# Part of a query convolution in 32x32 array tiles: sixteen-tile matmuls, a score product in four column tiles, and new order tables

## The chip, the cores and the metric

The kernel runs on one core of one Trainium2 chip. The metric is the device time of that core in microseconds: the median of 3 runs before was 682.94 us (681.64 to 685.73). The engines are named as in the profile: PE (TensorE, with PEld for its weight loads), DVE (VectorE), ACT (ScalarE), POOL (GpSimd) and SP (SyncE, which issues the DMAs).

## What is computed

Two layers over 4 images of 256 channels and 32x32 points, all in fp32. The reference, cut:

```python
# layer 0, x: (4, 256, 32, 32)
qkv = conv1x1(x, wq | wk | wv)                       # 768 channels
dw = conv5x5(qkv, dw_kernel, groups=768)             # depthwise, 25 taps
pw = conv1x1(dw, pw_kernel, groups=96)               # 8x8 blocks
f = concat([qkv, pw]).reshape(B, -1, 24, N)          # 64 heads of 8
query, key_, value = relu(f[:, :, :8]), relu(f[:, :, 8:16]), f[:, :, 16:]
scores = einsum('bhdn,bhen->bhde', [value, 1], key_)
out = einsum('bhde,bhen->bhdn', scores, query)
out = out[:, :, :-1] / (out[:, :, -1:] + EPS)
x = batchnorm(conv1x1(out, proj)) + x
# layer 1
norm = (x - mean) / sqrt(var + EPS)
attention = softmax(conv1x1(norm, f_w).T @ conv1x1(norm, g_w))   # 1024 x 1024
out = conv1x1(conv1x1(x, h_w) @ attention.T, o_w) + x
```

## The kernel before

The order of every engine is written out by hand; semaphores tie the engines together, and nothing is scheduled at run time. 768 qkv channels are six **tiles** of 128 channels, one channel to a partition: tiles 0 and 1 are queries, 2 and 3 keys, 4 and 5 values. `raw` holds a tile's image with a border; `conv` is the depthwise result, 25 taps (multiply by one weight per channel, shift, add) of 1024 points a tile.

The depthwise convolution is shared. DVE does whole taps (`conv_taps`, L1226), each multiplied and added in one instruction into two banks of PSUM: tiles 2, 3 and 0, and a part of tile 1. For tiles 4 and 5 and the rest of tile 1, ACT makes a product (`conv_products`, L965) into one of five buffers `prod`, and POOL adds it (`conv_adds`, L1485). Tile 1 is the **shared tile**: its first ten taps (`LATE`) are added on POOL into a second sum (`late_of`, tile `rows` or `q_raw` in the rows) and are done last; seven more are done by POOL in `conv`, eight by DVE. In the first batch POOL takes twelve and DVE three, and PE does all 25 taps of tile 5 itself: `diagonal_conv` (L551), 25 matmuls of 128x128 diagonal weights for each half image of 512 points. DVE builds these weights (L1445).

A batch's `body(b)` on PE starts when conv of tiles 2 to 5 is ready: eight slots of grouped 1x1 products and transposes for keys and values (`pwkv`, L735 and L737), which ACT drains into `kt` and `vt` (L979, L980); then qkv of the next batch (`raw_kv`), the scores (`scores`, L561: 8 or 9 blocks, two halves h, a full 128x129 product of which a mask keeps the 8x8 blocks), the query part (`pwq`, L750 and, for the late sum, L754), the raw keys, values and queries of the next batch, the denominators (L580) and their spread (L602), the projection (L779), layer 1's statistics (POOL's `rstd`, L1479) and its folded weights (L702, L712, L826), and last the attention: eight rows of energy (L667), transposes (L682) and values (L691). The 25-tap convolution of batch b+1 fills DVE, ACT and POOL all the while; tables (`TAPS_...`, `PRODUCTS_...`, `LATES_...`, `RSTD_AT`, `CARRY`) say how many taps, products and adds stand between the steps of a body. `CARRY` taps of batch b stand at the start of body b.

PSUM has eight banks: 0 to 3 turn round as **A slots** (PE fills one, ACT drains it: `a_full`, `a_free`), 4 and 5 as **D slots** for DVE, 6 and 7 hold DVE's convolution sum. In the attention the A banks hold energies and transposes. An fp32 matmul of the program stands in the trace as two pairs of a weight load and a matmul.

## Time and profile before

| | us |
|---|---|
| median of 3 runs | 682.94 |
| profiled execution | 682.24 |
| its span | 680.5 |
| PE busy | 627.4 |
| DVE busy | 563.8 |
| POOL busy | 541.8 |
| ACT busy | 468.9 |

The span is from the first to the last instruction; 1.7 us of the profiled execution lie around it. Busy time is a union of instructions; for PE it holds the latency of each matmul as well as the time that it feeds the array, so that a PE read as busy may be a little less full. The stages used below are cut where body(b) starts its `pwkv` (the first L735 of the batch) and where the attention of a batch starts (its first L667).

### The profile page before, as it was taken

How to read it: one execution, taken by the hardware profiler on the slowest of the kernel's cores; microseconds unless marked ns; L12 is line 12 of the kernel's file. 1: busy time of each engine (PE TensorE's matmuls, PEld its weight loads, DVE VectorE, ACT ScalarE, POOL GpSimd, SP SyncE). 2: the span in 40 equal slices, each digit the busy share in tenths (PEclk: the TensorE clock that was granted, in tenths of full speed). 3: DMA queues.
4: the chain of work that ended last, by engine and by line, in shares of the span. 5: the costliest groups of instructions: out<-in, count | busy, mean ns of one | idle time of the engine just before them, and what ended most of it. 6: DMA issues, size and time to landing. Idle time of an engine off the chain costs nothing.

```text
span 680.5 us, 8641 instructions
## 1 busy us (share of the span) xinstructions
PE 627.4 (92%) x3176; PEld 471.1 (69%) x3176; DVE 563.8 (83%) x661; ACT 468.9 (69%) x741; POOL 541.8 (80%) x253
## 2 busy tenths in 40 slices
PE   4979988999989998999989998999988978899998
PEld 3844547665868787765868797756767866478886
DVE  5899899898899999988889999879899998373321
ACT  4797619897787669788777769788767864233331
POOL 4999997999999999989999899999999987010000
PEclk9989989999999999999989999999999999999999
DMA  8000001000010000001010000000100000000000
GB/s 306 1 0 1 0 0 63 1 1 27 36 63 15 17 17 15 1 1 62 6 58 15 17 23 9 0 1 1 43 20 16 16 16 15 1 1 0 17 16 31
DMA packets 6537, 16.23 MB, mean 24 GB/s; under 512 B 864, under 2 KB 992, under 8 KB 5984
## 3 DMA queue, kind: packets, MB, share of 16 engines
q1 hardware_dynamic: 6496, 15.69, 6.5%
q8 instruction: 25, 0.41, 0.3%
q14 instruction: 16, 0.13, 0.1%
HBM read 11.50 MB, written 4.19 MB: 23 GB/s over the span
## 4 chain that ended last, share of the span: by engine, by line
PE 35%; issue 20%; DVE 16%; POOL 15%; ACT 12%; DMA 1%; SPq 0%; POOLq 0%; DVEq 0%; ACTq 0%
DVE ps L1226 9%; PE ps L667 8%; PE ps L691 8%; POOL rows L1485 7%; POOL conv L1485 7%; ACT prod L965 6%; PE ps L551 4%; DVE small L1410 3%; PE ps L826 2%; PE ps L682 2%; PE ps L484 2%; PE ps L636 2%; PE ps L485 1%; PE ps L488 1%; PE ps L702 1%
## 5 line engine op out<-in xcount | busy, mean ns | idle before, releaser
L1485 POOL TENSOR_TENSOR conv<-conv,prod 128x930 f32<-128x930 f32 (+4 forms) x197 | 432.6, 2239 | 14.9 <-ACT prod L965 12.0
L1226 DVE SCALAR_TENSOR_TENSOR ps<-raw,dw_sb,ps 128x930 f32<-128x930 f32 (+4 forms) x295 | 354.2, 1201 | 7.6
L965 ACT ACTIVATE prod<-raw,dw_sb 128x930 f32<-128x930 f32 (+4 forms) x233 | 250.1, 1122 | 17.3 <-POOL conv L1485 17.3
L691 PE MATMUL ps<-ht,pt 128*128 128x256 f32 x512 | 115.4, 379 | 2.7 <-ACT pt L1133 2.7
L691 PEld LDWEIGHTS ps<-ht,pt 128*128 128x128 f32 x512 | 95.0, 190 | 14.8 <-ACT pt L1133 3.1
L1124 ACT ACTIVATE rows<-ps,small 128x1024 f32<-128x1024 f32 x32 | 35.6, 1114 | 75.4 <-DVE small L1415 75.3
L1485 POOL TENSOR_TENSOR rows<-rows,prod 128x930 f32<-128x930 f32 (+4 forms) x27 | 62.7, 2321 | 7.5 <-ACT prod L965 4.0
L1410 DVE TENSOR_REDUCE small<-ps 128x1 f32<-128x1024 f32 x32 | 39.1, 1221 | 21.2 <-PE ps L667 21.0
L667 PE MATMUL ps<-hi,t_hi 128*128 128x512 f32 x128 | 44.6, 430 | 9.6 <-ACT rows L1124 9.5
L484 PE MATMUL ps<-hi,wqkv_hi 128*128 128x512 f32 x92 | 38.2, 416 | 4.1 <-ACT vt L980 4.1
L667 PE MATMUL ps<-lo,t_hi 128*128 128x512 f32 x128 | 40.4, 397 | 0.0
L979 ACT ACTIVATE kt<-ps 128x256 f32<-128x256 f32 x68 | 31.4, 465 | 10.4 <-PE ps L737 10.3
L485 PE MATMUL ps<-hi,wqkv_lo 128*128 128x512 f32 x92 | 36.6, 398 | 0.0
L682 PE MATMUL ps<-mask_sb,rows 128*128 128x128 f32 x256 | 33.5, 274 | 2.9 <-ACT pt L1133 2.7
L561 PE MATMUL ps<-vt,kt 128*128 128x129 f32 x272 | 32.1, 276 | 4.3 <-ACT vt L980 4.3
L667 PEld LDWEIGHTS ps<-hi,t_hi 128*128 128x128 f32 x128 | 23.5, 192 | 18.1 <-ACT rows L1124 13.0
L561 PEld LDWEIGHTS ps<-vt,kt 128*128 128x128 f32 x272 | 31.3, 192 | 6.5 <-ACT vt L980 5.8
L1428 DVE SCALAR_TENSOR_TENSOR x_t<-ps,small,x_t 128x256 f32<-128x256 f32 x32 | 15.1, 475 | 24.7 <-PE ps L691 24.7
L682 PEld LDWEIGHTS ps<-mask_sb,rows 128*128 128x128 f32 x256 | 29.1, 140 | 9.2 <-issue 3.8
L1133 ACT COPY pt<-ps 128x512 f32<-128x512 f32 x64 | 34.0, 586 | 1.1 <-PE ps L682 1.1
L667 PE MATMUL ps<-hi,t_lo 128*128 128x512 f32 x128 | 34.4, 390 | 0.0
L702 PE MATMUL ps<-oh_w,x 128*128 128x256 f32 x128 | 30.4, 382 | 2.1 <-DVE fold_lo L1391 2.1
(159 smaller groups left out, 1050.4 us busy)
## 6 DMA issues: line engine op xcount, KB each, us to landing
q_raw<-x_dram SPq DMA_DIRECT2D x8, 512.0 KB, 5.9
x<-x_dram SPq DMA_DIRECT2D x4, 1024.0 KB, 4.8
out_dram<-x_t SPq DMA_DIRECT2D x16, 256.0 KB, 2.3
conv<-wqkv_dram SPq DMA_DIRECT2D x1, 768.0 KB, 4.5
conv<-fg_dram SPq DMA_DIRECT2D x1, 512.0 KB, 5.7
proj_sb<-proj_dram SPq DMA_DIRECT2D x1, 512.0 KB, 7.3
pw_sb<-pw_dram SPq DMA_DIRECT2D x1, 384.0 KB, 6.5
mask_sb<-masks_dram SPq DMA_DIRECT2D x1, 264.0 KB, 6.3
```

The costliest lines, as they stand in the source:

```text
L484: pe.matmul(dst, lh, rh, start=(k == 0), stop=False)
L485: pe.matmul(dst, ll, rh, start=False, stop=False)
L561: mm = pe.matmul(dst[:, h * C:h * C + SCW], kt[:, j, h * P:(h + 1) * P], vt[:, j, h, 0:SCW], start=(j == 0), stop=(j == blocks - 1))
L667: mm = pe.matmul(ps[:, e_pair(b, i) + h, :], lhs, m[:, h * HALF:(h + 1) * HALF], start=(s == 0), stop=(s == len(steps) - 1))
L682: mm = pe.transpose(ps[:, T_PAIR + u, j * P:(j + 1) * P], rows[:, i % ROW_BUFS, key:key + P], ident)
L691: mm = pe.matmul(dst[:, 0:C], pt[:, i % PT_BUFS, j, :], ht[:, j, :], start=(j == 0), stop=(j == NB - 1))
L702: mm = pe.matmul(dst[:, i * C:(i + 1) * C], x1[:, k, n], oh_w[:, k, :], start=(k == 0), stop=(k == CK - 1))
L965: act.activation(dst, view, ACT.Copy, scale=weight(t, i)).then_inc(prod_ready, 1)
L1124: act.activation(rows[:, i % ROW_BUFS, :], ps[:, e_pair(b, i):e_pair(b, i) + 2, :].rearrange("p a n -> p (a n)"), ACT.Exp, bias=neg_max[:, ...
L1226: return dve.scalar_tensor_tensor(dst, view, w, before, ALU.mult, ALU.add)
L1410: dve.tensor_reduce(neg_max[:, i:i + 1], ps[:, e_pair(b, i):e_pair(b, i) + 2, :].rearrange("p a n -> p (a n)"), AX.X, ALU.max, negate=True ...
L1485: pool.tensor_tensor(total, total, product, ALU.add).then_inc(conv_pool, 1)
```

## The change

Three parts.

1. **Tap products in sixteen array tiles.** `diagonal_conv` is gone. A new `quads` gives four taps at a time to the 4x4 grid of 32x32 array tiles: row tile r holds channels 32r to 32r+31, column tile c one of four taps; weights are 32x32 diagonals. One such **wave** of 16 matmuls of 512 points does four taps of a half image, and leaves 4 x 4 partial results of 32 channels in four A banks (bank r: channels of group r, four column groups to be summed). ACT copies the four banks out (`sums`). A second product, `whole`, sums the column groups: four matmuls, each with 128 rows, 32 columns and 512 points. For tile 5 its weights are an identity; for queries they are the grouped 1x1 weights, so that it adds straight into the `pwq` product. In the first batch tile 5 goes this way whole (six waves and a quarter wave of 128 points a half) and tile 0 with 12 of its 25 taps (three waves); tile 1 with 16 taps in the first batch and 12 in the others. DVE no longer has taps of tile 1 at all; POOL keeps ten late ones (nine in the first batch) and three others (none in the first). DVE builds the smaller weights: three instructions of 800 columns at the start, one of 384 in each body with a next batch.
2. **Scores in column tiles.** Each 128x129 product becomes four of 32 columns and 33 points, one for each group of four heads; `vt` gets a ones column for each group.
3. **New tables**, now one row a batch; `CARRY` is 0. A DMA brings a second copy of the grouped weights (128 KB), and the residual x1 of the first batch is loaded after `pwq`, since x1 holds partial sums till then.

```diff
+QUAD_UNITS = [(5, 0), (5, 1), (0, 0), (0, 1)]
+LATE_OF = (9, 10, 10, 10)
+SHARED_OF = (0, 3, 3, 3)
+QUAD_OF = (16, 12, 12, 12)
-CARRY = (17, 16, 15, 2)
+CARRY = (0, 0, 0, 0)
-LATES_PWKV = (2, 1, 0, 1, 0, 0, 0, 1)
+LATES_PWKV = ((0, 0, 0, 0, 0, 0, 0, 4), (0, 0, 0, 0, 0, 0, 0, 3), (0, 0, 0, 0, 0, 0, 0, 3), (0, 0, 0, 0, 0, 0, 0, 2))
-RSTD_AT = (17, 18)
+RSTD_AT = ((12, 13), (13, 14), (16, 16))
+            def quads(slot, t, h, taps, weights):
+                waves = [taps[w:w + QUADS] for w in range(0, len(taps) - len(taps) % QUADS, QUADS)]
...
+                for w, (wave, places) in enumerate(waves):
+                    order = [(r, c) for r in range(QUADS) for c in range(QUADS)]
+                    for r, c in order if w == 0 else sorted(order, key=lambda rc: rc[1]):
+                        k, (y0, n_rows) = slice(r * QUAD, (r + 1) * QUAD), places[c]
+                        bank = a_slot(slot + r) if w == 0 and c == 0 else a_bank(slot + r)
+                        mm = pe.matmul(bank[c * QUAD:(c + 1) * QUAD, n0:n0 + n_rows * SIDE],
+                                       weights[k, TAP_ORDER[wave[c]], :], tap_view(t, wave[c])[k, y0:y0 + n_rows, :],
+                                       start=(w == 0), stop=(w == len(waves) - 1))
+                mm.then_inc(a_full, QUADS)
+            def whole(dst, weights, sums, start):
+                for r in range(QUADS):
+                    mm = pe.matmul(dst[r * QUAD:(r + 1) * QUAD, :], weights(r), quad_sums[sums][:, r, :],
+                                   start=start, stop=True)
             def scores(slot, kv_done, blocks):
...
-                        mm = pe.matmul(dst[:, h * C:h * C + SCW], kt[:, j, h * P:(h + 1) * P],
-                                       vt[:, j, h, 0:SCW], start=(j == 0), stop=(j == blocks - 1))
+                        for g in range(SUBS):
+                            m0 = h * P + g * SUB
+                            mm = pe.matmul(dst[g * SUB:(g + 1) * SUB, h * C:h * C + SCW], kt[:, j, m0:m0 + SUB],
+                                           vt[:, j, h * SUBS + g, :], start=(j == 0), stop=(j == blocks - 1))
             def body(b):
+                shared_quads(b, 0)
                 pe.wait_ge(conv_dve, dve_count(b, kv_taps(b)))
...
+                shared_quads(b, 1)
                 if with_next:
                     raw_kv(b + 1)
+            def sums(slot, h):
+                for r in range(QUADS):
+                    if r == 0:
+                        act.wait_ge(a_full, slot + QUADS)
+                    act.copy(quad_sums[h][:, r, :], a_bank(slot + r)).then_inc(a_free, 1)
```

On PE, between the raw queries of the first batch and its `pwkv`, there stood before (L551 is a tap of tile 5, L561 the scores, L580 the denominators, L602 their spread, L589 fused weights; the second row of taps shows the end of the first half image):

```order
L551 MATMUL ps<-raw,x 128x16x31
L561 MATMUL ps<-vt,kt 128x129 x18
L551 MATMUL ps<-raw,ht 128x512
L551 MATMUL ps<-raw,ht 128x16x30
L551 MATMUL ps<-raw,ht 128x16x31
L551 MATMUL ps<-raw,ht 128x512
L551 MATMUL ps<-raw,ht 128x16x31
L551 MATMUL ps<-raw,ht 128x16x30
L580 MATMUL ps<-q_raw,kd 32x256 x8
```

and now (L578 are tile matmuls of `quads`, 16 to a wave, L586 `whole`, L637 the scores, L656 the denominators, L665 fused weights, L678 the spread):

```order
L578 MATMUL ps<-raw,ht 32x512 x96
L578 MATMUL ps<-raw,ht 32x128 x16
L637 MATMUL ps<-vt,kt 32x33 x72
L578 MATMUL ps<-raw,ht 32x512 x96
L578 MATMUL ps<-raw,ht 32x128 x16
L586 MATMUL ps<-t_sums,mask_sb 32x512 x4
L656 MATMUL ps<-q_raw,kd 32x256 x8
L646 MATMUL ps<-mask_sb,s_masked 128x128 x2
L578 MATMUL ps<-raw,ht 32x512 x48
L586 MATMUL ps<-t_sums,mask_sb 32x512 x4
L665 MATMUL ps<-proj_sb,s_t 128x256 x2
L678 MATMUL ps<-den,mask_sb 128x256 x4
```

The 25 full-size taps of each half became waves of small ones, and the steps between them now stand behind whole groups of waves.

On ACT at the same place there stood before (L1192 batch norm's shift, L994 the copy of tile 5's result, L984 and L988 copies of small products, L965 products for POOL):

```order
L1192 ACTIVATE small<-small,bn_sb 128x1 x2
L994 COPY conv<-ps 128x512
L984 COPY s_t<-ps 128x256
L965 ACTIVATE prod<-raw,dw_sb 128x30x31
L965 ACTIVATE prod<-raw,dw_sb 128x30x30
L965 ACTIVATE prod<-raw,dw_sb 128x32x31
L988 COPY mb<-ps 128x512
L994 COPY conv<-ps 128x512
L979 ACTIVATE kt<-ps 128x256
```

and now, from the copy of the second group of partial sums on (L1063 the four copies of `sums`, L1078 of the whole result, L1032 products, L1051 and L1055 small products):

```order
L1063 COPY t_sums<-ps 128x512 x4
L1078 COPY conv<-ps 128x512
L1032 ACTIVATE prod<-raw,dw_sb 128x30x31
L1032 ACTIVATE prod<-raw,dw_sb 128x960
L1051 COPY s_t<-ps 128x256
L1032 ACTIVATE prod<-raw,dw_sb 128x30x31
L1063 COPY t_sums<-ps 128x512 x4
L1078 COPY conv<-ps 128x512
L1055 COPY mb<-ps 128x512
L1032 ACTIVATE prod<-raw,dw_sb 128x30x30
L1063 COPY t_sums<-ps 128x512 x4
```

Two copies became eighteen in the first batch's start, in groups of four.

On PE in body(0), from the scores to the transposes of the scores, there stood before (L570 are the transposes):

```order
L561 MATMUL ps<-vt,kt 128x129 x16
L750 MATMUL ps<-conv,pw_sb 128x512 x3
L754 MATMUL ps<-rows,pw_sb 128x512
L750 MATMUL ps<-conv,pw_sb 128x512
L754 MATMUL ps<-rows,pw_sb 128x512
L570 MATMUL ps<-mask_sb,s_masked 128x128 x2
```

and now (L616 and L620 are the products of `conv` and of the late sum, L646 the transposes; the names x and x_t are x1 and x1_t):

```order
L637 MATMUL ps<-vt,kt 32x33 x64
L616 MATMUL ps<-conv,pw_sb 128x512
L586 MATMUL ps<-t_sums,pw_sb 32x512 x4
L616 MATMUL ps<-conv,pw_sb 128x512
L586 MATMUL ps<-t_sums,pw_sb 32x512 x4
L620 MATMUL ps<-rows,pw_sb 128x512
L586 MATMUL ps<-x,pw_sb 32x512 x4
L620 MATMUL ps<-rows,pw_sb 128x512
L586 MATMUL ps<-x_t,pw_sb 32x512 x4
L646 MATMUL ps<-mask_sb,s_masked 128x128 x2
```

Sixteen score matmuls became 64 small ones, the two products of tile 1's `conv` went, and four `whole` products came; in later batches there are two.

## Rows read from the trace of the kernel before

**Rows 1.** The page: busy time by engine, and the span in slices.

```profile
PE 627.4 (92%) x3176; PEld 471.1 (69%) x3176; DVE 563.8 (83%) x661; ACT 468.9 (69%) x741; POOL 541.8 (80%) x253
DVE  5899899898899999988889999879899998373321
POOL 4999997999999999989999899999999987010000
```

**Rows 2.** Busy time by stage: stretch, length, each engine's busy time (instructions), clock.

```profile
0.00:49.30 49.30, 35.68 (x160) 28.53 (x160) 38.69 (x59) 35.57 (x57) 37.48 (x20) 0.93 0.30 106
49.30:102.70 53.40, 51.31 (x175) 25.88 (x176) 50.20 (x47) 26.66 (x32) 51.76 (x24) 0.97 0.00 1
102.70:189.90 87.20, 82.20 (x454) 60.12 (x453) 78.06 (x86) 75.12 (x128) 80.58 (x38) 1.00 0.09 27
189.90:340.00 150.10, 142.44 (x757) 110.02 (x757) 140.44 (x160) 120.53 (x188) 144.83 (x68) 1.00 0.06 21
490.80:554.90 64.10, 57.72 (x288) 46.25 (x287) 61.48 (x73) 46.29 (x63) 61.48 (x29) 1.00 0.07 25
554.90:620.40 65.50, 58.30 (x308) 41.41 (x308) 39.90 (x53) 26.58 (x56) 21.26 (x11) 1.00 0.02 9
620.40:680.50 60.10, 56.64 (x288) 48.41 (x286) 17.16 (x33) 18.02 (x33) 0.00 (x0) 0.99 0.05 18
```

**Rows 3.** Groups by line: xcount, busy us, mean ns, idle before and its releaser.

```profile
L1485 POOL TENSOR_TENSOR conv<-conv,prod 128x930 f32<-128x930 f32 (+4 forms) x197 | 432.6, 2239 | 14.9 <-ACT prod L965 12.0
L1226 DVE SCALAR_TENSOR_TENSOR ps<-raw,dw_sb,ps 128x930 f32<-128x930 f32 (+4 forms) x295 | 354.2, 1201 | 7.6
L965 ACT ACTIVATE prod<-raw,dw_sb 128x930 f32<-128x930 f32 (+4 forms) x233 | 250.1, 1122 | 17.3 <-POOL conv L1485 17.3
L561 PE MATMUL ps<-vt,kt 128*128 128x129 f32 x272 | 32.1, 276 | 4.3 <-ACT vt L980 4.3
L1445 DVE TENSOR_SCALAR ht<-mask_sb,dw_sb 128x128 f32<-128x128 f32 x16 | 3.2, 280 | 0.0
```

**Rows 4.** PE in order of time (start, us): taps of tile 5, then column tiles.

```profile
49.32 12.79 PE L551 MATMUL ps<-raw,ht 128*128 128x512 f32 x32 [1.17 <-ACT raw L934]
...
61.95 7.67 PE L551 MATMUL ps<-raw,x 128*128 128x512 f32 x18
...
78.58 0.42 PE L580 MATMUL ps<-q_raw,kd 128*32 128x256 f32 x4
...
78.58 1.07 PE L580 MATMUL ps<-q_raw,kd 128*32 128x256 f32 x16
```

**Rows 5.** PE in order of time: the densest run of small matmuls, one column each.

```profile
332.08 1.39 PE L826 MATMUL ps<-small,x 128*128 128x1 f32 x12
```

**Rows 6.** The chain of waits (start, us): what ACT takes to drain a bank.

```profile
321.41 0.47 ACT x_t L1025
321.87 1.01 ACT prod L965
...
419.22 1.08 ACT raw L934 x2
```

**Rows 7.** DVE and POOL in order of time, first batch: the last taps of tile 3.

```profile
82.69 1.28 DVE L1226 SCALAR_TENSOR_TENSOR conv<-raw,dw_sb,ps 128x1024 f32<-128x1024 f32 x1
59.79 24.46 POOL L1485 TENSOR_TENSOR conv<-conv,prod 128x961 f32<-128x961 f32 x11
84.20 4.67 POOL L378 TENSOR_TENSOR lo<-q_raw,hi 128x1024 fp32r<-128x1024 f32 x2
99.89 2.31 POOL L1485 TENSOR_TENSOR conv<-conv,prod 128x992 f32<-128x992 f32 x1
```

**Rows 8.** PE in order of time before the last batch's keys and values.

```profile
558.45 3.72 PE L691 MATMUL ps<-ht,pt 128*128 128x256 f32 x16 [2.69 <-ACT pt L1133]
562.01 0.61 PE L735 MATMUL ps<-pw_sb,conv 128*128 128x128 f32 x4
```

More of the change, by code:

```diff
@@ L33 @@
 RB = -(-SIDE * ROW // P)
-SCW = P + 1
+SUB = 32
+SUBS = P // SUB
+SCW = SUB + 1
 ROW_BUFS = 3
@@ new lines, with pool_order @@
+SHARED_REST = [[i for i in TAP_RANGE if i not in QUAD_SEQ[b]] for b in range(B)]
+FIRST_QUAD_SEQ = [i for i in TAP_RANGE if 1 <= i <= FIRST_QUAD_TAPS]
+LATE_SEQ = [[(SHARED_TILE, i) for i in SHARED_REST[b][:LATE_OF[b]]] for b in range(B)]
+SHARED_SEQ = [[(SHARED_TILE, i) for i in SHARED_REST[b][LATE_OF[b]:LATE_OF[b] + SHARED_OF[b]]] for b in range(B)]
+def pool_order(b):
+    own = [(t, i) for i in TAP_RANGE for t in (POOL_TILES if b else FIRST_POOL_TILES)]
+    for n, tap in enumerate(SHARED_SEQ[b]):
+        own.insert(SHARED_AT + 2 * n if b else SHARED_AT // 2 + n, tap)
+    return own
@@ new lines, in dve_order, with dve_seq @@
+def dve_order(b):
+    own = [(t, i) for t in (2, 3, 0) for i in TAP_RANGE if b or t or i not in FIRST_QUAD_SEQ]
+    return own + [(SHARED_TILE, i) for i in SHARED_REST[b][LATE_OF[b] + SHARED_OF[b]:]]
+POOL_SEQ = [pool_order(b) for b in range(B)]
+DVE_SEQ = [dve_order(b) for b in range(B)]
+POOL_STARTS = [[(t, 0) for t in POOL_TILES] + SHARED_SEQ[b][:1] for b in range(B)]
+ADD_SEQ = [[tap for tap in POOL_SEQ[b] if tap not in POOL_STARTS[b]] for b in range(B)]
+ALL_TAPS = 1000
+def dve_seq(b):
+    return DVE_SEQ[b]
@@ new lines, in pool_seq, with add_seq, late_seq, late_adds_of @@
+def pool_seq(b):
+    return POOL_SEQ[b]
+def add_seq(b):
+    return ADD_SEQ[b]
+def late_seq(b):
+    return LATE_SEQ[b]
+def late_adds_of(b):
+    return max(len(LATE_SEQ[b]) - 1, 0)
+def kv_taps(b):
+    return sum(t not in Q_TILES for t, _ in dve_seq(b))
+TAPS_SCORES_PW = (8, 10, 8)
+TAPS_DEN_PW = (4, 1, 5)
+TAPS_SCORES_RAW = (0, 2, 0)
+TAPS_DEN_RAW = (1, 0, 1)
+TAPS_Q_PW = ((1, 3), (0, 0), (1, 3))
+TAPS_PROJ = ((1, 0, 1, 0, 1, 0, 0, 2), (1, 0, 0, 0, 0, 0, 0, 1), (1, 0, 1, 0, 0, 0, 1, 1))
@@ new lines, in queries @@
+            def queries(b, t, h):
+                dst, cols, late = a_slot(A_AT["pwq", b] + 2 * t + h), slice(h * HALF, (h + 1) * HALF), t == SHARED_TILE
+                own = any(tap[0] == t for tap in DVE_SEQ[b] + POOL_SEQ[b])
+                last = [tap for tap in DVE_SEQ[b] if tap[0] == t][-1:]
+                if h == 0 and last:
+                    pe.wait_ge(conv_dve, dve_count(b, DVE_SEQ[b].index(last[0]) + 1))
+                if own:
+                    mm = pe.matmul(dst, pw_sb[:, t, :], conv[:, t, cols], start=True, stop=(b > 0 and not late))
+                if late and LATE_SEQ[b]:
+                    if h == 0:
+                        pe.wait_ge(conv_pool, late_add_count(b, late_adds_of(b)))
+                    pe.matmul(dst, pw_sb[:, t, :], late_of[b][:, cols], start=not own, stop=False)
+                if late or b == 0:
+                    if h == 0 and not late:
+                        pe.wait_ge(pw_quads_loaded, 16)
+                    pe.wait_ge(a_free, (A_AT[f"sums_{h}", b] if late else A_AT[f"first_{2 + h}", b]) + QUADS)
+                    mm = whole(dst, lambda r: pw_quad[:, t, r, :], h + (2 if late and b == 0 else 0),
+                               not own and not (late and LATE_SEQ[b]))
+                mm.then_inc(a_full, 1)
@@ L967, in late_products @@
             def late_products(b, first, last):
-                for n in range(first, min(last, LATE)):
+                for n in range(first, min(last, len(LATE_SEQ[b]))):
                     if n > 0:
                         act.wait_ge(conv_pool, late_add_count(b, n - PROD_BUFS))
-                    product(late_of[b] if n == 0 else product_buffer(late_add_count(b, n - 1)), *LATE_SEQ[n], n > 0)
+                    product(late_of[b] if n == 0 else product_buffer(late_add_count(b, n - 1)), *LATE_SEQ[b][n], n > 0)
             def keys_values(slot, j):
@@ L1441, in _ @@
             dve.tensor_scalar(bn_ve, var, BN_EPS, None, ALU.add).then_inc(bn_ve_ready, 1)
-            for t, i in PE_TAPS:
-                op = dve.tensor_scalar(diagonal(t, i), ident, weight(t, i), None, ALU.mult)
-            op.then_inc(diagonals_ready, 1)
+            for t in first_weights:
+                op = quad_products(first_weights[t], t, NTAPS)
+            op.then_inc(quad_weights_ready, 1)
             conv_taps(0, 0, FIRST_WEIGHTS)
```

442 lines of the change are left out of this document (216 added, 226 removed).

## The prediction

> **What bounds the kernel now.** I read the page's busy times first: PE 92%, DVE 83%, POOL 80% [rows 1]. The average hides two things. POOL and DVE stop at about 575 us, and the last 60 us are PE alone; up to there both are full in nearly every slice. So I cut the span into stages [rows 2]. A steady period, from one attention to the next, is 150.1 us and holds POOL 144.8, PE 142.4, DVE 140.4 and ACT 120.5. The adds of POOL stand 2.2 us each in an unbroken row, and ACT waits 17.3 us in all for POOL to free a product buffer [rows 3]. POOL is the fullest; but PE is only 2.4 us behind it. An engine relieved by 9 us uncovers the next at 2.
>
> The first batch is another case: from 49.3 to 102.7 us PE is busy 51.3 of 53.4, most of it with the 50 full-size taps of tile 5, of which 25 take 20.3 us [rows 2, 4]. POOL ends its adds for that batch at 102.2, just as early as PE, and DVE finished tile 3 at 84.0 [rows 7].
>
> **What goes from DVE, POOL and ACT.** DVE's taps for tile 1 are 8 a batch and 3 in the first, tile 0 loses 12 in the first: 15 x 1.20 = 18 us at the start, 9.6 us in each later batch, less about 0.5 for the new weight instruction. The 25 diagonal weights were 0.28 us each, 7 us [rows 3]; three instructions of 800 columns, by the taps' rate of 1.2 us for 930, are near 3. POOL loses 12 adds in the first batch (27 us) and 4 in each later one (4 x 2.24 = 9 us). ACT loses 13 products of 1.12 us, then 4 a batch, and gains 8 bank copies a batch of 0.5 us [rows 3, 6]: even, in the later batches.
>
> **What comes to PE.** A wave is 16 fp32 products of 512 points, two passes each. No row has sixteen array tiles; the nearest is the denominators, four column tiles. Sixteen matmuls of 256 columns take 1.07 us there with the tail; 16 of the same columns in one tile take 3.72 [rows 4, 8]. So the four run side by side, and one pass of 512 fp32 columns costs its 0.43 us whatever the number of tiles (25 x 2 matmuls in 20.3 us give 0.41). A wave is then 0.86 us, if loads and matmuls are issued quickly enough: 32 pairs, 27 ns each. From above a wave costs 32 x 0.115 = 3.7 us, should each pair cost what the densest run of tiny matmuls takes, 12 in 1.39 us [rows 5]; but those load 128 columns of weights in one tile one after another, and here they are 32 in sixteen. In the denominators the first four pairs start within 31 ns, 8 ns apart [rows 4]. I take 0.86. A `whole` is four column tiles of 512 points: 0.86 too.
>
> Each later batch thus gains six waves, 5.2 us, and two `whole`, 1.7. The first body gains four waves behind its start (3.4), four `whole` (3.4) and loses two products of 0.86.
>
> The scores: 68 pairs a batch of 129 points, 8.0 us of 32.1 in four [rows 3]. Now there are 272 pairs of 33 points, in four tiles. By points alone they cost under 2 us; at 28 ns a pair they cost what they did. Nothing in the trace shows a long run of such pairs. I take 14 ns, between the 8 ns of the start of the denominators and 28: 3.8 us, so -3.8 a batch, with 0 and -6 as bounds.
>
> **The exchange between PE and ACT.** Waves fill all four A banks at once, and ACT copies them only when all are full. Before, banks went round one by one. Each exchange leaves PE idle for the first copy, some 0.7 us, and the next group of waves has to wait for the last bank. In a later body there are two; late products of ACT now stand right behind the last keys and values, where ACT would wait for the waves anyway. I put 1.5 us a batch on it; from 0 to 5.
>
> In the first batch there are five groups in a row, with no other work for PE between them, and this sets the stage. Worked through from 49.3: ACT has three products, two copies of x and six small ones, till 56.5; four copies, 58.5; second group of 5.4 us, 63.9; ACT's five products meanwhile, copies till 67; the whole copy, three products and the scores' copy, 72; third group (2.6) from 70.3, copies and small products till 78; fourth, copies 82; four waves 85.6, first copy, 86.3. POOL is ready by then: 102.2 less 11 adds is 78, 3 more if it waits for x. DVE's keys are too, at 84.0 less 4 for the weights, plus 3.5 for a denominator and a scaling now ahead of them: 83.5. I take 88.5 for the start of body(0), **-14.2 us**; bounds 84 and 97 (2 us lost at every exchange).
>
> **The sum**, stage by stage against [rows 2]:
> - to 102.7: -14.2.
> - 102.7 to 189.9: waves +3.4, `whole` +3.4, product -1.7, scores -3.8, exchange +1.5, and relief -3: -0.2.
> - two steady periods: +5.2 +1.7 -3.8 +1.5 = +4.6 on PE; against it the idle time of PE that came from waits behind full DVE, POOL and ACT. The last attention, with no convolution beside it, takes 60.1 us where a steady one takes 65; PE's idle time in a period is 7.7. I take 6 of relief: -1.4 each, -2.8.
> - 490.8 to 620.4: the last attention beside a convolution runs to 562.0, 71 us, PE waiting 2.7 us at a time behind ACT's products [rows 8]. +5.2 +1.7 +1.5, scores -1.8, 1.6 hidden where PE idled after 562, relief -5: 0.
> - the last 60.1: the same.
>
> -17.2 us from 682.2: **665 us**. The profiled execution is 0.7 us under the median, nothing to correct. POOL and DVE are no longer the bound; PE is, at some 93 to 94% of the span.
>
> **A rule that speaks against it.** The first four matmuls of the denominators start within 31 ns in four column tiles [rows 4]. The Trainium skill ("TensorE: Matmul & The Clock Gate", Wait — 56ns, not 53.3ns?) says that start-to-start never falls below about 25 ns however few the columns; the trace does not agree for different tiles. By that rule a wave would still be hidden under its columns, and the scores would cost 272 x 25 = 6.8 us a batch, nearly as before; the sum would be about 677.
>
> **Rivals.**
> 1. *The issue of small pairs at 28 ns or a little more.* For it: no row shows a run of more than 16 such pairs, and a queue filled ahead can hide a slow issuer. Against it: the starts at 8 ns. The scores gain nothing, +15 us: 680. Chance 0.14.
> 2. *Slower: pairs issue at half that rate.* The sustained average in the denominators is 16 pairs in 0.86 us, 54 ns, though columns set it there. 44.5 waves are 1424 pairs, and the scores 1088; each ns above 27 costs 2.5 us. The gain is gone at 28 to 29 ns; at 54 it would be 680 + 2.5 x 27 = 748, some 735 with what the exchanges in the first batch hide. It decides in every `quads` of every body. Chance 0.10.
> 3. *The exchange costs full.* Eight groups in the bodies each leave PE idle for all four copies, 2 us rather than 0.7, and the ladder at the start ends at 92: 665 + 11 + 4 = 680. For it: PE has no slack now; against it: ACT has late products to fill with. Chance 0.12.
> 4. *The relief goes through whole.* POOL's and DVE's 9 us come back in each period, PE filling its gaps: 150 to 144, and 648. Against it: PE's own work grows. Chance 0.10.
> 5. *The forecast*, 655 to 676: 0.54.
>
> **Range and chances.** 645 to 686 leaves out the second rival and the tail of the fourth. 0.5% is 3.4 us, about what a measurement here tells from no change: faster means under 679.5. The forecast and the fourth are faster, and some four in ten of the first and third: 0.74. Same, half of those two: 0.12; slower, the second and the rest: 0.14.
>
> **What would show it.** L578 in the new trace: 96 matmuls of the program (192 in the trace) in 5.2 us right, over 7 wrong. L637: 72 in 2 us right, 4 rival 1, 8 rival 2. First L812 at 86 to 91 us. Period between first L743: 147 to 150. PE waiting for ACT's copies (L1063) 10 to 15 us in all; over 25 is rival 3. POOL idle over 18 us at the start of body(0), with no harm. If body(0) starts before 92 and the whole is still not faster, then PE's added work in the bodies was what I sized wrong.

## The result, and the profile after

| | before | after |
|---|---|---|
| time, median (us) | 682.8 (681.0 to 685.7, 6 runs) | 675.0 (670.6 to 678.2, 6 runs) |
| ratio | 1 | 0.9868, 95% interval 0.9839 to 0.9898 |
| profiled execution, time and span (us) | 682.2, 680.5 | 678.2, 676.4 |

The changed kernel is 1.3% faster, 7.8 us; 17.2 were forecast. Its profiled execution is the slowest of its six, so the traces differ by 4 us only. The kernel before with four-column scores was profiled in a slow execution (690.1 us, where its median is 683.1), so the length of its stages and its clock are not compared with the others below.

The page of the kernel after: busy time, the granted clock in 40 slices, and the chain that ended last, by engine.

```profile
PE 631.8 (93%) x5456; PEld 461.4 (68%) x5456; DVE 523.8 (77%) x603; ACT 469.8 (69%) x764; POOL 487.3 (72%) x229
PEclk9899999999899999999899999998989999999999
PE 71%; DVE 10%; issue 7%; ACT 7%; POOL 2%; DMA 1%; SPq 0%; DVEq 0%; POOLq 0%; ACTq 0%
```

POOL fell from 541.8 to 487.3 us and DVE from 563.8 to 523.8 [rows 1]. TensorE is busy for 4 us more. Of the chain that ended last, 71% is TensorE's own work, where before it was 35%, with DVE 16% and POOL 15%.

Windows of the kernel after, cut like [rows 2], without the first stretch and the one from 487.1 to 616.1 us (stretch, length, busy time of PE, PEld, DVE, ACT, POOL with instructions, granted clock, DMA):

```profile
49.30:85.44 36.14, 31.96 (x850) 15.68 (x833) 35.05 (x34) 22.65 (x39) 30.72 (x14) 1.00 0.01 3
85.44:174.09 88.65, 84.60 (x812) 57.25 (x813) 68.56 (x78) 71.25 (x126) 63.70 (x31) 1.00 0.08 26
174.09:328.27 154.18, 147.97 (x1169) 109.18 (x1168) 125.06 (x146) 122.89 (x195) 140.08 (x66) 0.99 0.06 22
328.27:487.14 158.87, 149.89 (x1170) 111.01 (x1168) 145.07 (x160) 123.82 (x195) 139.61 (x66) 0.97 0.04 14
616.14:676.40 60.26, 57.10 (x289) 48.69 (x287) 17.16 (x33) 18.15 (x33) 0.00 (x0) 1.00 0.05 18
```

The start is 17.2 us shorter: body(0) begins at 85.44 instead of 102.67. The steady periods give it back: 154.2 and 158.9 us, against 150.1 and 151.4 before. In the first of them POOL has 4.8 us less work than before and DVE 15.4 less, and the period is 4 us longer; TensorE is busy 148.0 of it, 5.5 more. In the second DVE is not relieved at all: it is busy for 145.1 us, 6.8 of them in one weight instruction, where it was 138.5 before, and it does 79 taps where it did 80, since the new tables put work of other stages there. The last stage is as it was.

From here on I measure a period from one first pointwise product (L812; L735 before) to the next, since it is found in every kernel; "tail" is from the last one to the end of the span. Light kernels have only 14 of 32 rows of the convolution on DVE, POOL and ACT in batches 1 to 3.

| kernel | start | period 0 | 1 | 2 | tail |
|---|---|---|---|---|---|
| before | 102.7 | 150.9 | 151.4 | 157.1 | 118.5 |
| after | 85.4 | 157.6 | 153.4 | 160.3 | 119.7 |
| before, four-column scores (execution of 690.1 us) | 102.2 | 156.9 | 153.8 | 157.0 | 118.5 |
| after, full scores | 86.2 | 162.8 | 157.3 | 157.6 | 122.0 |
| after, weights by ACT | 85.6 | 160.9 | 152.1 | 153.1 | 121.5 |
| waves in the first batch only | 85.8 | 158.5 | 149.9 | 160.5 | 118.4 |
| the same, second tables | 85.2 | 156.5 | 153.9 | 160.7 | 118.6 |
| two waves, four carried taps | 85.0 | 158.6 | 155.9 | 158.2 | 127.6 |
| no later waves, twelve carried taps | 85.5 | 156.4 | 162.6 | 170.5 | 137.1 |
| before, light | 104.3 | 149.1 | 144.8 | 146.6 | 117.0 |
| after, light | 84.8 | 155.1 | 151.2 | 152.8 | 119.7 |
| after, light, no later waves | 85.0 | 152.9 | 141.0 | 139.7 | 114.3 |
| after, light, one wave | 85.2 | 156.4 | 150.5 | 148.8 | 119.4 |
| waves in first and last batch | 85.6 | 156.0 | 150.3 | 149.8 | 120.1 |

Three sizes were disputed ahead. A group of three waves, one for each half (PE in order of time, kernel after):

```profile
238.82 3.41 PE L578 MATMUL ps<-raw,mb 32*32 32x512 f32 x96
242.99 0.68 PE L812 MATMUL ps<-pw_sb,conv 128*128 128x128 f32 x4 [0.77 <-POOL conv L1580]
...
248.48 4.01 PE L578 MATMUL ps<-raw,mb 32*32 32x512 f32 x96
253.25 0.47 PE L512 MATMUL ps<-hi,wqkv_hi 128*128 128x512 f32 x1 [0.77 <-ACT t_sums L1063]
```

and the first of the two score products of a batch, 64 program matmuls in four column tiles (128 in the trace; the second product, of the raw keys and values, has 72):

```profile
264.62 1.30 PE L637 MATMUL ps<-vt,kt 128*32 128x33 f32 x128
```

The matmuls of the first group start within 2.82 us, 0.94 a wave; one matmul lasts 0.59 us, so sixteen array tiles do run side by side. Those of the second group take 3.42 us from first to last start, since it has to wait for ACT to drain the banks of the pointwise products (its weight loads wait 0.5 us for `vt`). And from its start to the next work a group takes 4.2 and 4.8 us. The 128 score matmuls take 1.10 us from first to last start, about 8.6 ns a start. A steady batch has 272 of them, 2.3 us, where its 68 full matmuls took 7.6: 5.3 us are saved.

### The profile page after: what moved, and what is told of

Same layout as the page of the kernel before. It is cut to its first block, busy times and chain, and to the rows that moved or that the text cites. A ratio compares the mean times of both kernels' runs of the same rounds, so it can differ in the third digit from the quotient of the medians.

```text
span 676.4 us, 13121 instructions
## 1 busy us (share of the span) xinstructions
PE 631.8 (93%) x5456; PEld 461.4 (68%) x5456; DVE 523.8 (77%) x603; ACT 469.8 (69%) x764; POOL 487.3 (72%) x229
## 4 chain that ended last, share of the span: by engine, by line
PE 71%; DVE 10%; issue 7%; ACT 7%; POOL 2%; DMA 1%; SPq 0%; DVEq 0%; POOLq 0%; ACTq 0%
PE ps L767 12%; PE ps L743 10%; PE ps L578 7%; PE ps L846 5%; PE ps L512 4%; PE ps L516 3%; PE ps L513 3%; PE ps L758 3%; DVE ps L1317 3%; PE ps L778 2%; PE ps L812 2%; ACT prod L1032 2%; POOL conv L1580 2%; PE ps L586 2%; PE ps L893 2%
## 5 line engine op out<-in xcount | busy, mean ns | idle before, releaser
L1580 POOL TENSOR_TENSOR conv<-conv,prod 128x930 f32<-128x930 f32 (+4 forms) x174 | 382.8, 2239 | 59.8 <-ACT prod L1032 57.1
L1317 DVE SCALAR_TENSOR_TENSOR ps<-raw,dw_sb,ps 128x930 f32<-128x930 f32 (+4 forms) x264 | 317.0, 1201 | 6.8
L1032 ACT ACTIVATE prod<-raw,dw_sb 128x961 f32<-128x961 f32 (+4 forms) x209 | 217.1, 1101 | 1.2 <-POOL conv L1580 1.2
L1580 POOL TENSOR_TENSOR rows<-rows,prod 128x930 f32<-128x930 f32 (+4 forms) x26 | 58.2, 2240 | 17.1 <-ACT prod L1032 13.6
L743 PE MATMUL ps<-hi,t_hi 128*128 128x512 f32 x128 | 46.8, 448 | 7.0 <-ACT rows L1210 7.0
L743 PE MATMUL ps<-lo,t_hi 128*128 128x512 f32 x128 | 41.7, 407 | 0.0
L1523 DVE SCALAR_TENSOR_TENSOR x_t<-ps,small,x_t 128x256 f32<-128x256 f32 x32 | 15.2, 476 | 30.8 <-PE ps L767 30.8
L743 PE MATMUL ps<-hi,t_lo 128*128 128x512 f32 x128 | 35.1, 397 | 0.0
L1063 ACT COPY t_sums<-ps 128x512 f32<-128x512 f32 x40 | 20.5, 600 | 21.0 <-PE ps L578 21.0
L1001 ACT COPY raw<-ps 128x512 f32<-128x512 f32 x48 | 28.4, 615 | 8.2 <-PE ps L547 4.0
L743 PEld LDWEIGHTS ps<-hi,t_hi 128*128 128x128 f32 x128 | 24.6, 198 | 13.7 <-ACT rows L1210 9.1
L1046 ACT ACTIVATE kt<-ps 128x256 f32<-128x256 f32 x68 | 28.9, 426 | 1.6 <-PE ps L561 1.2
```

The source lines that it names most:

```text
L743: mm = pe.matmul(ps[:, e_pair(b, i) + h, :], lhs, m[:, h * HALF:(h + 1) * HALF], start=(s == 0), stop=(s == len(steps) - 1))
L1032: act.activation(dst, view, ACT.Copy, scale=weight(t, i)).then_inc(prod_ready, 1)
L1317: return dve.scalar_tensor_tensor(dst, view, w, before, ALU.mult, ALU.add)
L1580: pool.tensor_tensor(total, total, product, ALU.add).then_inc(conv_pool, 1)
```

## Experiments

### One part alone, one part undone: the scores

The kernel before with the new scores, and the kernel after with the old ones:

```diff
-                        mm = pe.matmul(dst[:, h * C:h * C + SCW], kt[:, j, h * P:(h + 1) * P],
-                                       vt[:, j, h, 0:SCW], start=(j == 0), stop=(j == blocks - 1))
+                        for g in range(SUBS):
+                            m0 = h * P + g * SUB
+                            mm = pe.matmul(dst[g * SUB:(g + 1) * SUB, h * C:h * C + SCW], kt[:, j, m0:m0 + SUB],
+                                           vt[:, j, h * SUBS + g, :], start=(j == 0), stop=(j == blocks - 1))
```

> The kernel before with one part of the change alone: the scores in four column tiles of 32 columns of keys (L561 of before turned into four matmuls of 33 points each). In the profile of after 64 program pairs of this form take 1.10 us, against 112 ns for each of 68 full ones before: TensorE is relieved of 5.3 us in each steady period, 2 to 3 in the first and the last batch, 18 in all. Theory A, that TensorE's own stream sets the steady periods: the periods fall from 150 to about 145 and the time from 682.8 to 665 or so. Theory B, that POOL and DVE (144.8 and 140.4 us of work in 150.1) set them in the kernel before: TensorE waits elsewhere for what it has saved, the periods stay at 148 to 150, the time at 677 to 682.

Measured 683.1 us, 0.9977 of before (0.9951 to 1.0002): no difference that can be told, and 1 us above what theory B allowed. The window of period 1, of which only the busy times are used here (the execution took 690.1 us):

```profile
259.03:412.82 153.79, 142.84 (x961) 107.28 (x960) 140.36 (x159) 120.19 (x188) 144.96 (x68) 0.97 0.06 22
```

> The kernel after with the scores back in their old form (128 columns of keys, 129 points, one tile), everything else as it is. Theory A, TensorE's own stream sets the periods of the kernel after: +5.3 us a steady period, +2.5 in the last batch, +2 at the start, 675 to about 692. Theory B, the periods after are set by waits for DVE, POOL and ACT (order tables, full engines): the 5.3 us disappear in waits, 676 to 681.

Measured 686.8 us, 1.0042 of before (1.0012 to 1.0072). Against after's 0.9868 that is 0.0174, 12 us of the 18 of work that came back. The same edit is worth nothing in one kernel and 12 us in the other. In the kernel before, less work on TensorE shortens nothing: POOL and DVE have 145 and 140 us in each period whatever TensorE does (theory B there). A part may be the clock: nine of ten executions with the new scores were granted 0.977 to 0.987 over the span, the kernel before 0.980 to 0.997 (medians 0.982 and 0.989), but no run separates the two. In the kernel after, TensorE's work counts (theory A, for two thirds).

### VectorE's weight instruction

```diff
-                if with_next:
-                    quad_products(later_weights, SHARED_TILE, QUAD_OF[b + 1]).then_inc(quad_weights_ready, 1)
...
+                    for tap in taps:
+                        mm = act.activation(later_weights[:, tap, :], quad_ident, ACT.Copy,
+                                            scale=dw_sb[:, SHARED_TILE, tap:tap + 1])
```

> The kernel after, but the 12 weights of tile 1 for the next batch are written by ScalarE, three small copies after each of four row blocks of the attention, and not by VectorE's one instruction with two inputs in SBUF (L1342), which took 0.55, 1.70 and 6.78 us in the three bodies of the profiled execution. Theory: the third one is held up by GpSimd's adds and holds back the fold, on which TensorE waited 4.6 us, with the granted clock at 0.87 behind it: the period of body(1) to body(2) falls from 158.9 to 153 to 155, the time by 3 to 6 us to 669 to 672, and the runs lie closer together than 670.6 to 678.2. Rival: the wait belongs to the order tables of that batch (the power instruction of GpSimd stands behind 16 adds there), or the copies cost ScalarE in the attention what they save: within 1 us of 675.

Why it was made: DVE and POOL of the kernel after in order of time, at the third such instruction.

```profile
461.28 0.68 DVE L1460 TENSOR_TENSOR lo<-ps,hi 128x512 fp32r<-128x512 f32 x1
461.88 1.18 DVE L1317 SCALAR_TENSOR_TENSOR ps<-raw,dw_sb,ps 128x930 f32<-128x930 f32 x1
462.97 6.78 DVE L1342 TENSOR_TENSOR mb<-mask_sb,dw_sb 128x384 f32<-128x384 f32 x1
469.68 1.28 DVE L1469 TENSOR_TENSOR ht<-ps,oh_b 128x512 f32<-128x512 f32 x2
```

```profile
461.73 1.10 POOL L1574 TENSOR_TENSOR small<-small 128x1 f32<-128x1 f32 x2
462.76 6.58 POOL L1580 TENSOR_TENSOR conv<-conv,prod 128x961 f32<-128x961 f32 x3
```

The weight instruction (L1342) ends 0.4 us behind POOL's third add. Then the waits between 460 and 487 us, and the granted clock behind them (window 470 to 475, where 0.60 stands):

```profile
PEld ps L788 <- DVE ht L1469: 4.7, 1, 4.7
PE ps L788 <- DVE ht L1469: 4.6, 1, 4.6
```

```profile
470.00:475.00 5.00, 4.59 (x17) 3.87 (x17) 3.83 (x7) 1.50 (x3) 0.00 (x0) 0.60 0.00 0
```

With the weights on ScalarE, period 2 is 153.1 instead of 160.3, and the windows of periods 1 and 2 show TensorE busy for 146.7 and 146.5 us. But period 0 is 3.3 longer and the tail 1.8, and the whole is 674.8 us, 0.9837 (0.981 to 0.9864), against after's 0.9868: in the median some 2 us, inside the intervals. The wait was that instruction's and not the tables', which settles the rival's first half; the rest stays inside the intervals.

### What relief is worth at all

The same instructions of the convolution, each with less than half of the rows:

```diff
+        def crop(image, b):
+
+            return image[:, 0:14, :] if b else image
```

> The kernel before with the convolution work of DVE, POOL and ACT in batches 1 to 3 cropped to 14 of 32 rows (the output of those batches lacks the rest): the same instructions in the same order, each about half as long, TensorE's work unchanged. It measures what full relief of these engines is worth, in the kernel in which the forecast took POOL for the bound. Theory A, that most of TensorE's 7.7 us of idle time in a period are turnarounds with ACT and DVE inside the attention and the chain behind the projection, and not waits behind full engines: the periods fall from 150 by 2 to 4 us only, to 146 to 148, the attention stays at 63 to 65 us. Theory B, the forecast's relief of 6 us a period in full: 144 or less, the attention at 60 to 61.

> The kernel after with the same crop (14 of 32 rows on DVE, POOL and ACT in batches 1 to 3, the rest of the output left out; waves and everything else of TensorE whole). Theory A, the kernel after is TensorE's own stream: the periods, 154.2 and 158.9 in the profiled execution, become 151 to 153, and the attention stages, first L743 to the first wave, stay at 63 to 65. Theory B, the engines beside it still set them (order tables, the weight instruction, GpSimd's port): 145 to 148.

The windows of period 1, kernel before light, then after light:

```profile
253.35:398.19 144.84, 141.17 (x758) 110.21 (x757) 96.38 (x159) 93.45 (x188) 74.53 (x67) 1.00 0.07 23
```

```profile
239.89:391.09 151.20, 146.28 (x1168) 108.25 (x1169) 93.36 (x154) 95.84 (x193) 71.43 (x64) 1.00 0.06 22
```

665.4 us (0.9742, 0.9691 to 0.9794) and 667.2 us (0.977, 0.9718 to 0.9821), of two runs each. POOL has 75 and 71 us of work in a period and DVE under 97, so what is left is TensorE's stream with its own turnarounds. For before my theory gave too little for the later periods: relief is worth 6.6 and 10.5 us in periods 1 and 2. In period 1 the attention falls from 65.1 to 62.1 us and the body by 3.5. For after it was right: TensorE's stream needs 151.2 us.

Cut at the start of each attention, as the forecast was, the same traces give (us):

| kernel | body(0) | steady 1 | steady 2 | last beside a convolution, and its body |
|---|---|---|---|---|
| before | 87.1 | 150.1 | 151.4 | 128.8 |
| before, light | 85.4 | 146.4 | 144.9 | 120.5 |
| difference | 1.7 | 3.7 | 6.6 | 8.4 |
| after | 88.7 | 154.2 | 158.9 | 129.0 |
| after, light | 88.6 | 151.2 | 151.3 | 127.5 |
| difference | 0.1 | 3.0 | 7.6 | 1.5 |

The difference is what waiting for full engines costs. The light kernels give TensorE's **floor**, its own work with its turnarounds, and the change raised it by 3.2, 4.8, 6.4 and 7.0 us. The waiting fell in body(0) and above all in the last stage, by 6.9 us, but hardly at all in the two steady periods. In the whole, by medians, the kernel before stands 17.4 us above its floor and the kernel after 7.8. What sets the 150 to 151 us of a steady period before isn't shown: TensorE's floor is 144.9, POOL's busy time 144.8 to 145.0, and both lie well below it.

### Where TensorE's 6.4 us come from

```diff
             def shared_quads(b, h):
 
+                if b:
+                    return
```

with the copies of the sums and the whole products left out in the same way; and, for one wave,

```diff
-                quads(A_AT[f"sums_{h}", b], SHARED_TILE, h, QUAD_SEQ[b], later_weights if b else ...)
+                quads(A_AT[f"sums_{h}", b], SHARED_TILE, h, QUAD_SEQ[b][:QUADS if b else NTAPS], later_weights if b else ...)
```

> The kernel of after with DVE, POOL and ACT relieved (14 of 32 rows, as before), and in batches 1 to 3 no waves, no copies of their sums and no whole products: the 12 taps of tile 1 that TensorE had there are left out. In the relieved kernels TensorE's stream alone sets the periods: 151.2 us after, 144.8 before (first pwkv to first pwkv, second period). This one gives what the waves cost in all. Theory, the exchange was sized too low: 144.8 less 5.3 for the scores is 139.5, so waves with everything that they bring cost 11.7 us a batch, of which 6.2 are the waves as the trace shows them (2.82 and 3.42), 1 the whole products and 4.5 the exchange with ACT. Rival, the exchange is the 1.5 us of the forecast, and the 5.3 us of the scores don't shorten the stream (they are given back as waits or as a lower granted clock): 142 to 143.

> The same relieved kernel with one wave of four taps instead of three for each half in batches 1 to 3 (8 taps left out), sums and whole products kept. It splits the cost of the waves into what goes with their number and what is paid once. Theory: 4 half-waves of 0.94 us fewer, 3.8 us a batch, 147.4 for the second period, so that 7.9 of the 11.7 us are paid however many taps are taken. Rival, the exchange goes away with the number of waves (ACT copies while TensorE still computes): 144 or less.

```profile
237.93:378.96 141.03, 137.64 (x961) 106.03 (x960) 93.32 (x153) 91.87 (x184) 72.44 (x65) 0.99 0.07 23
```

```profile
241.50:392.01 150.51, 145.04 (x1040) 108.16 (x1041) 93.38 (x154) 95.69 (x193) 72.34 (x65) 0.98 0.06 22
```

635.4 us and 660.9 us, two runs each. Without waves the period is 141.0 and then 139.7: the waves with all they bring cost 10.2 and 13.1 us, 11.7 as a mean, as the theory said; over the whole span it is 30.7 us for three batches, so 10.2 a batch. PE of the light kernel after in order of time shows the parts:

```profile
235.72 3.41 PE L582 MATMUL ps<-raw,mb 32*32 32x512 f32 x96
239.89 0.68 PE L816 MATMUL ps<-pw_sb,conv 128*128 128x128 f32 x4 [0.77 <-POOL rows L1586]
...
245.38 4.01 PE L582 MATMUL ps<-raw,mb 32*32 32x512 f32 x96
250.16 0.47 PE L516 MATMUL ps<-hi,wqkv_hi 128*128 128x512 f32 x1 [0.77 <-ACT t_sums L1067]
...
261.52 1.30 PE L641 MATMUL ps<-vt,kt 128*32 128x33 f32 x128
...
270.29 0.44 PE L650 MATMUL ps<-mask_sb,s_masked 128*128 128x128 f32 x2
```

and the same place without waves:

```profile
237.93 0.61 PE L819 MATMUL ps<-pw_sb,conv 128*128 128x128 f32 x4
...
243.17 0.48 PE L517 MATMUL ps<-hi,wqkv_hi 128*128 128x512 f32 x1
...
254.54 1.30 PE L644 MATMUL ps<-vt,kt 128*32 128x33 f32 x128
...
261.02 0.38 PE L653 MATMUL ps<-mask_sb,s_masked 128*128 128x128 f32 x2
```

The first group takes 4.17 us (235.72 to 239.89). From the first pointwise product to the next batch's first image it is 10.27 against 5.24, so the second group costs 5.03. From the scores to the transposes, 8.77 against 6.48: the two whole products cost 2.3. Together 11.5. Of the two groups' 9.2 us, 7.4 are the busy time of the waves (6.2 from the first to the last start of each group, the rest the length of its last matmuls) and 1.5 the idle time of 0.77 us behind each.

With one wave the periods are 150.5 and 148.8, only 0.7 and 4.0 below those with three, where 3.8 was expected. PE then waits 1.17 us for ACT's copies, and the clock falls behind the wait (windows of 5 us around the second group):

```profile
247.00:252.00 5.00, 3.83 (x38) 2.05 (x38) 4.75 (x8) 4.33 (x10) 3.33 (x3) 0.80 0.02 3
252.00:257.00 5.00, 5.00 (x20) 4.01 (x19) 0.94 (x2) 3.30 (x6) 2.49 (x4) 0.86 0.00 0
```

Leaving out eight of the twelve taps gives TensorE back 2.3 us a period as a mean (2.1 a batch by the medians of the whole); the other four carry about 9. This kernel's clock was 0.984 over the span, the light kernel after's 0.997, which is the likely reason for the missing 1.5 us, but no run shows the one without the other.

### Fewer waves later

The kernels of this section have their whole output again. First the new start and scores with the old shares and tables in batches 1 to 3:

```diff
-QUAD_OF = (16, 12, 12, 12)
+QUAD_OF = (16, 0, 0, 0)
-SHARED_OF = (0, 3, 3, 3)
+SHARED_OF = (0, 7, 7, 7)
-CARRY = (0, 0, 0, 0)
+CARRY = (0, 16, 15, 2)
```

> The kernel after with the waves in the first batch alone: 16 taps of tile 1, tile 5 and 12 taps of tile 0 on TensorE there, scores in four column tiles, but in batches 1 to 3 no waves, no whole products, no weight instruction; DVE, POOL and ACT have their taps of before there (8, 7 and 10 of tile 1) in the order tables of before. Start as after: first L812 at about 85.4. If the waves of the later batches are paid by TensorE and relieve nobody who is waited for (theory A), the periods fall to 145 to 150 against 154.2 and 158.9: 675 goes to 655 to 662. If POOL and DVE full again set the periods (theory B, the relief of the forecast was real), they are 150 or more and the time is 665 to 670, or over 675 if the relief of 6 us a period was there in full.

672.4 us, 0.9817 (0.9791 to 0.9843): some 3.5 us below after. The waves of batches 1 to 3, with the tables made for them, gained nothing; whether they lost is at the edge of what the intervals tell, which touch. It misses theory A's 655 to 662, and lies above theory B's 665 to 670 as well:

```profile
244.26:394.19 149.93, 139.59 (x961) 105.38 (x960) 140.31 (x159) 120.30 (x188) 144.60 (x68) 0.99 0.06 22
```

The period is 150 again, with 144.6 us of adds on POOL and TensorE idle for 10 us.

Then taps given back to DVE, at the start of the body, with ACT writing the weights and after's tables otherwise:

```diff
-QUAD_OF = (16, 12, 12, 12)
-CARRY = (0, 0, 0, 0)
+QUAD_OF = (16, 8, 8, 8)        (second kernel: 16, 0, 0, 0)
+CARRY = (0, 4, 4, 4)           (second kernel: 0, 12, 12, 12)
```

> The kernel after with two waves instead of three for each half in batches 1 to 3 (8 taps of tile 1 on TensorE), the 4 taps given back to DVE and carried into the start of the body, where it waits for the scores; weights of the waves by ScalarE as in the run before this. Tables otherwise those of after. TensorE has 1.9 us less in a batch, DVE 4.8 more at a place where it was idle. Theory A (TensorE's stream sets the periods): 4 to 6 us less than the kernel after with ScalarE's weights, 669 to 671. Theory B (others set them): no change, 674 to 676, or worse.

> The same with no waves at all in batches 1 to 3: 12 taps of tile 1 carried by DVE at the start of the body (14.4 us), POOL and ACT with the 3 and 10 taps of after in the tables of after, no copies of the sums, no whole products there. TensorE has 7.5 us less in a batch. Theory A: 18 to 22 us less than the kernel after, 653 to 658. Theory B, GpSimd (140 us of work in a period) or the chain behind DVE's carried taps takes over as the bound: 662 to 670, periods near 147 to 150.

Both fell far outside: 692.1 us (1.0124, 1.0089 to 1.0159) and 715.8 us (1.0466, 1.0431 to 1.0502). "Where it was idle" was not read from a row. DVE of the second kernel around the start of body(1), at 241.9:

```profile
249.97 12.31 DVE L1322 SCALAR_TENSOR_TENSOR ps<-raw,dw_sb,ps 128x930 f32<-128x930 f32 x10
262.32 1.28 DVE L1322 SCALAR_TENSOR_TENSOR conv<-raw,dw_sb,ps 128x1024 f32<-128x1024 f32 x1
263.69 3.42 DVE L1322 SCALAR_TENSOR_TENSOR ps<-raw,dw_sb,conv 128x1024 f32<-128x1024 f32 x1
267.15 12.33 DVE L1322 SCALAR_TENSOR_TENSOR ps<-raw,dw_sb,ps 128x930 f32<-128x930 f32 x10
```

```profile
PE ps L619 <- DVE conv L1322: 15.5, 2, 15.2
```

After's tables leave tile 0's last taps for the end of the attention; DVE works at them till 263.6, and the carried ones come behind. TensorE's products for the queries wait 15.2 us, and over this period it is granted 0.92 of its clock. These two say nothing on the waves. The second shows that DVE has no room at this place; for the first, with four carried taps, the cause isn't shown.

Last, the first of these kernels with two taps moved from POOL to DVE and fewer products of ACT in the stretch of the next batch's images:

```diff
-SHARED_OF = (0, 7, 7, 7)
-PRODUCTS_KVT = ((0, 1, 0, 0, 0, 1, 1, 0, 1), ...)
+SHARED_OF = (0, 5, 5, 5)
+PRODUCTS_KVT = ((0, 1, 0, 0, 0, 1, 0, 0, 0), ...)
...
```

> Waves in the first batch only, as the run of 672.4 us (0.9817 of before), with two taps of tile 1 moved from POOL to DVE in batches 1 to 3 (5 and 10 instead of 7 and 8) and four of ACT's products taken out of the stretch in which it copies the next batch's images and keys and put before and behind it. POOL, the fullest at 144.6 of 150.0 us, loses 4.5, DVE gains 2.4 to 142.7, and TensorE waits less for ACT there (it waited 3.3 us of ten, and its clock stood at 0.64 to 0.84 behind that). Theory B, these engines set the periods when there are no waves: 2 to 4 us a period less, 662 to 667. Rival, TensorE's own turnarounds: within 1.5 us of 672.

677.2 us (0.991, 0.9876 to 0.9945): 5 to 6 us worse than the tables it started from. POOL has 140.3 us in period 1, as meant, and the period is 153.9 instead of 149.9. A lower sum on the fullest engine gave nothing, so POOL's sum alone doesn't set these periods. Since the run changed two things at once, the share of taps and the order, which of them did the harm isn't told.

### A version that beats both

Waves in the first and in the last batch, where waiting for DVE, POOL and ACT cost most (8.4 us in the stage before the last); shares and tables of before in batches 1 and 2; weights by ACT (the edit, cut; the tables follow it):

```diff
-QUAD_OF = (16, 12, 12, 12)
-SHARED_OF = (0, 3, 3, 3)
+QUAD_OF = (16, 0, 0, 12)
+SHARED_OF = (0, 7, 7, 3)
```

> Waves where TensorE has slack or where the engines beside it are late, and nowhere else: in the first batch (as after) and in the last, with the tables and shares of after for batch 3 and ScalarE's weights; batches 1 and 2 without waves, in shares and tables of before. The stages up to the second attention are those of the run with waves in the first batch only (394.2 us to the third first pwkv); from there on the kernel after with ScalarE's weights needed 274.6 us to the end, the other 278.8, its last attention beside a convolution 72.3 against 68.0. Theory (a group of waves costs TensorE 11 to 12 us a batch, of which 8 or more are paid once, and is worth that only where DVE, POOL and ACT are waited for anyway): a span of 665 to 669, 666 to 671 us, below both the kernel after (675) and the run with waves in the first batch only (672.4). Rival: the gain of 4 us in the last stage is lost again at the seam between the two kinds of tables (DVE enters body(2) with 15 carried taps, for which after's tables have no room): 672 to 677.

665.1 us (663.6 to 668.5), 0.9751 of before (0.9709 to 0.9793). Its interval lies wholly under after's; that of waves in the first batch only (from 0.9791) it touches at its end, but the slowest of its six runs (668.5) is faster than the fastest of the other's six (669.8). Period 2:

```profile
391.81:541.61 149.80, 142.59 (x1057) 107.24 (x1056) 139.38 (x162) 123.91 (x202) 140.77 (x66) 0.99 0.04 15
```

It was 160.3 in the kernel after, 153.1 there with the weights by ACT, as here, and 160.5 with waves in the first batch only: in this body no waves of batch 2 stand on TensorE, and the convolution prepared beside it is the relieved one of batch 3. The seam between the tables cost nothing visible.

## Why the prediction was right, and where it was not

The direction and the range held; the size, 7.8 us of 17.2, did not. That the range held was in part luck: in the profiled executions the start came out 3.0 us better than forecast, TensorE's added work behind it 4.4 us dearer, and the relief 12 us short. By its steps:

- **Start to body(0)**, -14.2: measured -17.2, at 85.4, within the bounds of 84 and 97, but not by the ladder as I had drawn it. The first two groups took 7.00 and 7.92 us of busy time, where I had 5.4 for each. The ladder began earlier: the first group starts at 45.15 us, before the cut at 49.3, and ACT's first four copies stand at 52.2 to 54.2 us instead of 56.5 to 58.5.

```profile
45.15 7.00 PE L578 MATMUL ps<-raw,ht 32*32 32x512 f32 x224 [1.47 <-ACT raw L1001]
54.77 7.92 PE L578 MATMUL ps<-raw,ht 32*32 32x512 f32 x224
```

```profile
52.19 2.05 ACT L1063 COPY t_sums<-ps 128x512 f32<-128x512 f32 x4 [0.79 <-PE ps L578]
```

- **Scores**, 14 ns a pair, -3.8 a batch: 8.6 ns, -5.3. The right side of the bounds, a size off. The rule of the Trainium skill ("TensorE: Matmul & The Clock Gate", Wait — 56ns, not 53.3ns?), that start-to-start doesn't fall below some 25 ns, isn't borne out here for matmuls of different column tiles: 128 in 1.10 us. Rival 1 fell with this.
- **Waves and whole products**, 0.86 us each: sized too low. By the mark I had set, the 192 matmuls of a batch in 5.2 us right and over 7 wrong, they are wrong: 7.4 us of busy time. The first group starts a wave every 0.94 us, the second, held up by banks that ACT still drains, every 1.14, and each group ends with 0.59 us of its last matmuls. The pair of whole products costs 2.3 us instead of 1.7. Rival 2, 54 ns a pair, was too slow all the same: 192 start in 6.2 us, 33 ns each.
- **The exchange**, 1.5 us a batch: as forecast, twice 0.77 us of idle time. In the whole kernel after, PE waits 6 us for the copies of L1063, where I had set 10 to 15. Rival 3 was near in sum (680 forecast, 675 measured), but by its own mark, over 25 us of such waits, it is wrong. Behind the first group of a batch the profile names POOL as the one that came last in one case of three.
- **Relief**, -6 a steady period: this is the term that failed. There was about so much waiting to be had in the kernel before, 3.7 and 6.6 us in the two steady periods, but the kernel after still waits 3.0 and 7.6 in them, so that nothing came back. POOL loses 9 us of adds a batch, as I had it, but only 4.8 and 5.4 of that in the steady periods; its sum there is still 140 us. DVE loses 15.4 us in the first and nothing in the second. I had taken the relief of a whole batch for the relief of every window, and not read where the new tables put the work. In the second period the weight instruction adds to it: with the weights by ACT it takes 152.3 us, 1.1 above the floor, and the first 155.1. In the last stage the relief came in full, 6.9 us for the 5 forecast, and in body(0) 1.6 for 3.
- **TensorE's additions**, by the light kernels: +3.2 in body(0), +4.8 and +6.4 in the steady periods, +7.0 in the last stage, where the sum has +2.8, +4.6, +4.6 and +5. The waves and whole products were dearer, the scores cheaper.
- **The weight instruction**, "about 0.5": 0.55, 1.70 and 6.78 us in the profiled execution. The last cost period 2 some 7 us there; in the median of all runs 2 or so.
- **Comparing with the last attention**: I took its 60.1 us against 65 as room that a relieved period would get. But with half of the convolution beside it a steady one still takes 62 to 64. The code of the last attention differs, with two energy buffers and no spreads between its rows, which is the likely rest; no run separates it.
- **What would show it**: the periods between first L743, 147 to 150 forecast, are 154.2 and 158.9. The last sentence there, that PE's added work was sized wrong if body(0) starts before 92 and the whole is still not faster, names only the smaller part: the added work was 4.4 us off, the relief 12.

## What to carry to other kernels

When two engines are within a few per cent of each other, work out where each stage gets its relief, window by window and from the new order of the work, not from the sum over a batch. Work out each engine's floor too, its own work with its turnarounds; halving the work beside it measures that floor directly. A period is at least the larger floor, and here it was longer: 151.4 us, with TensorE's floor at 144.9 and 145 us of work on POOL. Count a group that fills all banks with its start, its end and its hand-over, not by its matmuls: here about 9 us were paid for the first four taps and 2 to 4 for the next eight, so such groups belong where the others are waited for. And before moving work to "where an engine is idle", read the row of that place.
